# Slot norm statistics moved from GpSimd to VectorE, one token group's norm done earlier, the expert start and a filler moved

## The reference

```python
x = x + _L0_xattn_ref(_layernorm(x, axis=-1), ctx_1024, L0_xattn_Wq, L0_xattn_Wkv, L0_xattn_Wo)
x = x + _L0_ffn_ref(_layernorm(x, axis=-1), L0_ffn_norm_g, ...)
...
def _L0_ffn_ref(x, norm_g, norm_b, slot_g, slot_b, scale, slot_embeds, Wg, bg, Wu, bu, Wd, bd):
    x = _layernorm(x, norm_g, norm_b)
    se = _layernorm(slot_embeds, slot_g, slot_b) * scale
    logits = jnp.einsum('bnd,esd->bnes', x, se)
    dispatch = jax.nn.softmax(logits, axis=1)
    combine = jax.nn.softmax(logits.reshape(x.shape[0], x.shape[1], -1), axis=-1)
    slots = jnp.einsum('bnd,bnes->besd', x, dispatch)
    gate = jax.nn.gelu(jnp.einsum('besd,edf->besf', slots, Wg) + bg[None, :, None, :], approximate=False)
    up = jnp.einsum('besd,edf->besf', slots, Wu) + bu[None, :, None, :]
    eout = jnp.einsum('besf,efo->beso', gate * up, Wd) + bd[None, :, None, :]
    eout = eout.reshape(eout.shape[0], -1, eout.shape[-1])
    return jnp.einsum('bns,bso->bno', combine, eout)
```

## Time and profile before

| | us |
|---|---|
| time, median of 3 runs | 936.28 (935.89 to 938.46) |
| time of the profiled execution | 936.28 |
| its span (first to last instruction) | 934.6 |

### The profile page before, as it was taken

The page is one execution under the profiler, slowest core; times in us unless marked ns, Lnnn a source line. Parts: engine busy times, 40 slices in busy tenths (PEclk is TensorE's granted clock), DMA queues, the critical chain, the costliest instruction groups (busy, mean ns, idle before and its releaser), DMA issues.

```text
span 934.6 us, 16084 instructions
## 1 busy us (share of the span) xinstructions
PE 877.7 (94%) x4768; PEld 675.4 (72%) x4768; DVE 703.1 (75%) x1613; ACT 525.4 (56%) x1008; POOL 584.4 (63%) x575
## 2 busy tenths in 40 slices
PE   7898999999898888999999999999999999998897
PEld 5566666666597856788888888888888676776675
DVE  6997777999645789866666666666668778887866
ACT  3555667544561165666666666666666755446365
POOL 5922444677802245777777777777777778988600
PEclk9999999999999999999999999999999989999998
DMA  7000000322000000200000000000002000000001
GB/s 200 1 2 1 0 2 0 96 68 67 28 2 29 1 9 2 68 26 26 25 25 21 24 25 23 25 25 25 25 21 98 1 1 1 1 1 1 0 13 35
DMA packets 27432, 24.46 MB, mean 26 GB/s; under 512 B 3483, under 2 KB 24179, under 8 KB 27251
## 3 DMA queue, kind: packets, MB, share of 16 engines
q1 hardware_dynamic: 27379, 23.80, 8.6%
HBM read 22.74 MB, written 1.05 MB: 25 GB/s over the span
## 4 chain that ended last, share of the span: by engine, by line
PE 68%; DVE 18%; POOL 6%; ACT 5%; issue 3%; DMA 0%; DVEq 0%; POOLq 0%; ACTq 0%
PE psum L1909 63%; POOL hh L744 3%; DVE arena L1842 2%; ACT hh L876 2%; DVE stats L1369 1%; PE psum L2077 1%; DVE arena L1477 1%; DVE arena L1474 1%; ACT arena L937 1%; PE psum L1970 1%; DVE xn L1388 1%; POOL rstd L655 1%; PE psum L2154 1%; PE psum L1939 1%; DVE arena L1486 1%
## 5 line engine op out<-in xcount | busy, mean ns | idle before, releaser
L1909 PE MATMUL psum<-xw 128*128 128x512 f32 x1248 | 323.0, 394 | 2.6 <-POOL xw L667 1.1
L707 POOL TENSOR_TENSOR hh<-arena,hh 128x512 fp32r<-128x512 f32 x176 | 228.1, 1296 | 81.7 <-ACT hh L876 80.3
L1909 PEld LDWEIGHTS psum<-xw 128*128 128x128 f32 x1248 | 232.2, 188 | 55.1 <-issue 3.8
L1740 DVE TENSOR_TENSOR psum<-psum,arena 128x512 f32<-128x512 f32 x176 | 123.0, 699 | 97.8 <-PE psum L1909 91.5
L1108 ACT ACTIVATE arena<-psum 128x512 f32<-128x512 f32 x176 | 105.4, 599 | 120.3 <-PE psum L1909 120.2
L876 ACT ACTIVATE hh<-arena 128x512 fp32r<-128x512 f32 x228 | 142.3, 625 | 38.5 <-DVE arena L1842 36.1
L1909 PE MATMUL psum<-hh,wdn 128*128 128x512 f32 x528 | 148.3, 389 | 0.2 <-POOL hh L707 0.2
L1745 DVE TENSOR_TENSOR arena<-psum,arena 128x512 f32<-128x512 f32 x176 | 121.7, 691 | 7.6 <-DVE psum L1740 1.7
L1909 PEld LDWEIGHTS psum<-hh,wdn 128*128 128x128 f32 x528 | 98.9, 188 | 21.1 <-POOL hh L707 0.5
L1909 PE MATMUL psum<-arena 128*32 128x128 f32 (+6 forms) x992 | 90.1, 313 | 10.1 <-ACT arena L876 6.8
L876 ACT ACTIVATE arena<-psum 128x512 f32<-128x512 f32 (+6 forms) x85 | 57.4, 687 | 48.6 <-PE psum L1970 18.6
(11 more groups left out here) (296 smaller groups left out, 1494.9 us busy)
## 6 DMA issues: line engine op xcount, KB each, us to landing
egu<-in_w SPq DMA_DIRECT2D x44, 128.0 KB, 2.1
egu<-in_egu SPq DMA_DIRECT2D x16, 256.0 KB, 2.7
edn<-in_w SPq DMA_DIRECT2D x44, 64.0 KB, 1.8
edn<-in_edn SPq DMA_DIRECT2D x16, 128.0 KB, 2.0
arena<-in_w SPq DMA_DIRECT2D x1, 1536.0 KB, 6.5
X<-in_x SPq DMA_DIRECT2D x4, 256.0 KB, 4.2
arena<-in_ctxTd SPq DMA_DIRECT2D x2, 512.0 KB, 5.8
arena<-in_conv SPq DMA_DIRECT2D x1, 768.0 KB, 4.3
```

Of the source, the lines that this page charges most:

```text
L707: pool.tensor_tensor(hh[:, s % 4, 1, :], h1[:, s % 2, :], hh[:, s % 4, 0, :].bitcast(F32), ALU.subtract).then_inc(hh_lo, 1)
L1740: dve.tensor_tensor(bank(2 + k), bank(2 + k), sil[:, k, :], ALU.mult).then_inc(prod_done, 1)
L1909: return pe.matmul(dst, lhsT=lhsT, rhs=rhs, start=start, stop=stop)
```

## The change

- `slot_sums` and its passes leave GpSimd. VectorE makes the slots' statistics at `t == 5` of the attention loop (`slot_stats`: 8 BN_STATS, 8 BN_AGGR, one TENSOR_SCALAR), then `slot_gs`. GpSimd waits for them (`se_var`) and keeps the power, one subtraction and one product.
- Group 3's statistics are made as for other groups, right behind tile 15's residual addition; its power moves to behind step 3 on GpSimd, its application to `q == 6`, its transposes and evacuation to `q == 9`. Group 2's evacuation moves to behind `bexp(0)`.
- `bmax(2)` stands ahead of `brec(0)`.
- At the experts' start VectorE and TensorE wait for all 16 slot evacuations (15 before on VectorE; TensorE's wait stood in `least_T(0)`). ScalarE's first weight copy moves behind the last evacuation, and the Gelu table is no longer loaded ahead of time by a dummy activation.
- `busy(6, 3)` is added at the head of `combine_rows2`.

The first copy and the table load now stand behind the last evacuation. The diff:

```diff
@@ -163,8 +163,8 @@
         ctxTd = carve(B * 2 * C)
         slot_raw = carve(ES // P, D)
         slot_n = carve(ES // P, D)
-        slot_sq = carve(ES // P, D)
-        slot_half = carve(ES // P, D // 2)
+        smv = carve(ES // P, 2)
+        sstats = carve(ES // P, 6)
         srstd = carve(3, ES // P)
         taken[0] = 0
@@ -323,6 +323,7 @@
         ln_xn = sem("ln_xn")
         ln_tp = sem("ln_tp")
         ln_xnT = sem("ln_xnT")
+        se_var = sem("se_var")
         se_n = sem("se_n")
         se_tp = sem("se_tp")
         se_T = sem("se_T")
@@ -798,22 +799,9 @@
                     ln_power(0, 3)
                     for b in range(4, B):
                         keys(b)
-
-                    def slot_sums(rows):
-                        then(pool.tensor_tensor(slot_half, rows[:, :, 0:D // 2], rows[:, :, D // 2:D], ALU.add))
-                        n = D // 4
-                        while n:
-                            then(pool.tensor_tensor(slot_half[:, :, 0:n], slot_half[:, :, 0:n], slot_half[:, :, n:2 * n], ALU.add))
-                            n //= 2
-
-                    pool.wait_ge(w_slots, 16 * N_SLOTS)
-                    slot_sums(slot_raw)
-                    then(pool.tensor_scalar(srstd[:, 2, :], slot_half[:, :, 0], 1.0 / D, None, ALU.mult))
-                    then(pool.tensor_tensor(slot_n, slot_raw, wide(srstd[:, 2, :].unsqueeze(2), ES // P, D), ALU.subtract))
-                    then(pool.tensor_tensor(slot_sq, slot_n, slot_n, ALU.mult))
-                    slot_sums(slot_sq)
-                    then(pool.tensor_scalar(srstd[:, 0, :], slot_half[:, :, 0], 1.0 / D, EPS, ALU.mult, ALU.add))
+                    pool.wait_ge(se_var, 1)
                     then(pool.tensor_tensor(srstd[:, 1, :], srstd[:, 0, :], neghalf[:, 0:ES // P], ALU.pow))
+                    then(pool.tensor_tensor(slot_n, slot_raw, wide(smv[:, :, 0:1], ES // P, D), ALU.subtract))
                     pool.tensor_tensor(slot_n, slot_n, wide(srstd[:, 1, :].unsqueeze(2), ES // P, D), ALU.mult).then_inc(se_n, 1)
                     continue
                 for g in range(NG):
@@ -825,7 +813,7 @@
                         pool.wait_ge(brec_done, k + 1)
                         pool.tensor_tensor(qb[:, k % 4], qb[:, k % 4], wide(recB[:, k % 4].unsqueeze(2), 2, N), ALU.mult)\
                             .then_inc(bnorm_done, 1)
-                        if k == 7:
+                        if k == 3:
                             ln_power(1, NG - 1)
                     experts0_low()
                     pool.wait_ge(xh_lo, E0)
@@ -955,13 +943,6 @@
                                           bias=nmB[:, k % 4, c:c + 1], accum_out=sumB[:, k % 4, c:c + 1])
                 last.then_inc(bexp_done, 1)
-            def gate_up0_high(n, i, k, f):
-
-                act.wait_ge(egu_in[k], i * 16 + 16)
-                if later(n, 2):
-                    act.wait_ge(eu_ready, n - 1)
-                copy(wgu_pair(f, 0), egu_part(k, f)).then_inc(wgu_hi, 1)
-
             def slots_evac(b, hf):
                 act.wait_ge(slots_mm, 2 * b + hf + 1)
                 act.activation(slotsT[:, 8 * hf:8 * hf + 8, b, :], bank(6 + hf).rearrange("p (e s) -> p e s", s=S0), ACT.Identity,
@@ -970,22 +951,26 @@
 
             bexp(0)
+            ln_evac_group(1, 2)
             bexp(1)
             bexp(2)
             for q in range(4 * B + 2):
                 if q + 3 < 4 * B:
                     bexp(q + 3)
-                if q in (4, 14):
-                    ln_evac_group(1, 2 if q == 4 else NG - 1)
-                if q == 4 * B - 4:
-                    gate_up0_high(0, 0, 0, 0)
-                if q == 4 * B - 2:
-                    load_table(ACT.Gelu)
+                if q == 9:
+                    ln_evac_group(1, NG - 1)
                 if q >= 4 and q % 4 == 1:
                     slots_evac(q // 4 - 1, 1)
                 if q % 4 == 3 and q < 4 * B:
                     slots_evac(q // 4, 0)
+
+            def gate_up0_high(n, i, k, f):
+
+                act.wait_ge(egu_in[k], i * 16 + 16)
+                if later(n, 2):
+                    act.wait_ge(eu_ready, n - 1)
+                copy(wgu_pair(f, 0), egu_part(k, f)).then_inc(wgu_hi, 1)
             def gelu(n, e, f):
                 act.wait_ge(eg_ready, n + 1)
@@ -1032,6 +1017,7 @@
                             eo_low(i - 2)
                 row_evac(i)
+            gate_up0_high(0, 0, 0, 0)
             expert_pair(0)
             expert_pair(1)
             with act.Fori(2, E0 // 2 - 1) as i:
@@ -1393,7 +1379,7 @@
                 if L == 7 and t == NT - 1:
                     token_low(0)
-                if t % 4 == 3 and not (L == 1 and t == NT - 1):
+                if t % 4 == 3:
                     if L == 7 and t // 4 == 2:
                         token_integers(0)
                     ln_stats(L, t // 4)
@@ -1448,6 +1434,17 @@
                     .then_inc(xq_lo, 1)
 
+            def slot_stats():
+                dve.wait_ge(w_slots, 16 * N_SLOTS)
+                for t in range(ES // P):
+                    last = dve.bn_stats(sstats[:, t, :], slot_raw[:, t, :])
+                then(last)
+                for t in range(ES // P):
+                    last = dve.bn_aggr(smv[:, t, :], sstats[:, t, :])
+                then(last)
+                dve.tensor_scalar(srstd[:, 0, :], smv[:, :, 1], EPS, None, ALU.add).then_inc(se_var, 1)
+                dve.tensor_scalar(slot_gs[:, :], cols[:, COL["slot_g"]:COL["slot_g"] + 2], scal[:, 0:1], None, ALU.mult).then_inc(se_n, 1)
+
             ln_stats(0, 0)
             ln_apply(0, 0)
             dve.wait_ge(krep_done, 1)
@@ -1478,8 +1475,7 @@
                 if t in (0, 2):
                     ln_stats(0, 2 + t // 2)
                 if t == 5:
-                    dve.wait_ge(w_slots, 16 * N_SLOTS)
-                    dve.tensor_scalar(slot_gs[:, :], cols[:, COL["slot_g"]:COL["slot_g"] + 2], scal[:, 0:1], None, ALU.mult).then_inc(se_n, 1)
+                    slot_stats()
                 if 2 <= t <= NT + 1:
                     u = t - 2
                     dve.wait_ge(av_ready, u + 1)
@@ -1510,17 +1506,15 @@
 
             bmax(1)
+            bmax(2)
             brec(0)
-            bmax(2)
             for q in range(4 * B):
                 if q + 1 < 4 * B:
                     brec(q + 1)
                 qt_evac(q // 4, q % 4)
                 if q + 3 < 4 * B:
                     bmax(q + 3)
-                if q == 4:
-                    ln_stats(1, NG - 1)
-                if q == 10:
+                if q == 6:
                     ln_apply(1, NG - 1)
             def slot_halves(e, k):
@@ -1571,10 +1565,9 @@
                         if f == 0 and k == 0 and later(i, 2):
                             eo_high(i - 2)
-            dve.wait_ge(slots_sb, 2 * B - 1)
+            dve.wait_ge(slots_sb, 2 * B)
             slot_halves(0, 0)
             slot_halves(1, 1)
-            dve.wait_ge(slots_mm, 2 * B)
             least_logits(0)
             expert_pair(0)
             expert_pair(1)
@@ -2100,10 +2093,12 @@
                     dispatch_T(q)
                     if q + 3 < 4 * B:
                         logits_slots(q + 3)
-                if q == 14:
+                if q == 9:
                     ln_transpose(1, NG - 1)
                 if q >= 2:
                     slots_part((q - 2) // 4, (q - 2) % 4 // 2, q % 2)
+
+            pe.wait_ge(slots_sb, 2 * B)
             def gate_up0(n, k, f):
@@ -2127,8 +2122,6 @@
             def least_T(b):
                 pe.wait_ge(least_done, b * 4 + 3)
-                if not later(b, 1):
-                    pe.wait_ge(slots_sb, 2 * B)
                 if later(b, 2):
                     pe.wait_ge(eo_tok[1], b - 1)
                 for a in range(TB):
@@ -2521,6 +2514,7 @@
                 mm(bank(4 + q), w2part(0, c, 1), hh[:, n % 4, 1, :], False, c == NC2 - 1).then_inc(down_done, 1)
             def combine_rows2():
+                busy(6, 3)
                 pe.wait_ge(rw_done, NG + 1)
                 for q in range(2):
                     half = bank(4 + 3 * q).bitcast(BF16)
```

## The result

| | before | changed |
|---|---|---|
| time, median of 5 runs each, us | 936.28 (932.58 to 938.46) | 942.40 (940.88 to 942.61) |
| profiled execution: time, us | 936.28 | 941.85 |
| its span, us | 934.6 | 940.1 |
| mean granted TensorE clock | 0.978 | 0.978 |

The ratio is 1.0065, with a 95% interval from 1.0052 to 1.0079: the changed kernel is slower by 6.1 us, 4.9 to 7.4.

A forecast was written before the change was run, and what follows sets the result against it. VectorE was taken to bound layer 0's attention and the experts' start, TensorE the dispatch loop and layer 5's routing transposes. 1.1 + 0.9 + 2.2 + 0.7 = 4.9 us on 936.28 gave 941.2 us, 8-in-10 range 938.9 to 943.4.

The forecast's parts named there:

- A: Slot statistics on VectorE in layer 0's attention: 1.1 us slower, after the refund from a shorter slot_gs.
- what is added to VectorE here is paid in full: Layer 0's attention: VectorE sets the pace, so its added work costs its full length; GpSimd's work beside it costs nothing.
- the clock rival: TensorE's clock falls in new idles at the dispatch ramp (942.7 us) and experts' start (943.3 us); 22%.
- B: Group 3's norm and bmax order at the dispatch ramp: 1.53 us later, 0.59 refunded, 0.9 us net.
- C: Experts' start: 1.91 us waiting for the 16th evacuation plus 0.3 for copies beside slot halves, 2.2 us; bounds 1.9 and 2.6.
- Table load: Gelu table at the experts' start: its 1.28 us load runs during TensorE's first gate product, cost 0.
- D: Filler busy(6, 3) ahead of layer 5's routing transposes, where TensorE is late: 0.7 us, bounds 0 and 1.3.
- Nothing gives the delay back: Stages between the changed places: no engine waits for something with a fixed time, so the 4.9 us delay stays.
- The overlap at the start: Experts' start: TensorE's 1.13 us idle is slack of the whole stage, so 1.1 us there and 940.1 in all; 14%.
- The clock staying up: Low-clock stretches at 82 to 84 and 778 us vanish: 938.3 us, within 0.3% of before; 12%.

The follow-up runs named there:

- the kernel without C: Changed kernel with VectorE waiting for 15 evacuations again, first weight copy, Gelu table and TensorE's wait at their old places: 939.86 us, ratio 1.0043 to before.
- the kernel without A: Changed kernel with slot statistics back on GpSimd and slot_gs alone on VectorE at t == 5: 939.63 us, ratio 1.0042 to before.

## Why the prediction came out as it did

**Direction, range: right**, and by its mechanism; that the number came so close is partly luck, as the last but one paragraph says. VectorE's added work in layer 0, the shifted ramp and the 16th evacuation are paid one behind the other, and no stage hides one.

**A: mis-sized.** The sum "2.5 + 0.1 - 1.46 = 1.1 us" was right in its own terms (1.18). The step that failed is "what is added to VectorE here is paid in full" taken as all there is to pay. A step of 3.70 us on VectorE is an idle of 2.36 on TensorE, and behind it came half clock in the stage where TensorE has little slack: 1.42 more, and 0.25 at the second stretch. The prediction had the clock rival for the ramp and the experts alone, though the attention loop had the row that showed such a fall.

**B: right**, 1.54 and back 0.6 to 0.67, net 0.87 against 0.9. The clock fall behind the 2.30 us idle is the first rival's; it stands in the changed kernel's profile and that of the kernel without C (0.8 us), and not in three others with the same idle. It was priced at 942.7 - 941.2 = 1.5, twice what it took.

**C: wait right, contention too small.** 1.91 as worked out; 0.3 was taken for the copies beside the slot halves, 0.63 was measured here, with TensorE at half clock, and 1.00 to 1.01 in the four kernels with both copies late and full clock. So the bound of 2.6 for C was too low: at full clock C is 2.9. The clock rival's "at most 0.6" more for a fall at the experts didn't come either: with the fall the stretch was shorter, 5.91 against 6.29. "Between 0 and 0.73 I take 0.3" counted one copy; the pair falls there. The rule of the Trainium skill (SBUF — State Buffer, Who interferes with whom), an exclusive hold by whoever comes first, is nearer: GpSimd's first operation begins at 165.90 and would be done with its 0.73 at 166.63; VectorE's, issued at 166.02, ends at 167.18, 0.55 us behind that. The trace agrees in the order of who waits, and not to the last tenth: a hold to the end would let VectorE's 0.69 us end at 167.32. VectorE pays 0.4 to 0.5 at each collision.

**Table load: right**, no cost. **D:** 0.7 predicted, 0.76 in the row, 0.5 in the difference.

**"Nothing gives the delay back": wrong.** The 7.08 us at `hidden0(0)` are 7.12 at the end of the experts (255.86 against 249.51, and 0.77) and 6.02 at the `up2` products (5.25 + 0.77); with D's 0.50 and 0.26 back behind it they are 6.26 at the end (5.49 + 0.77). In the part where 1.1 came back, both profiles have four stretches' length of half clock, at other places (from 258, 299, 312 and 336 us before; from 263, 317 and, twice as long, 341 in the changed kernel). In the last part the changed kernel has none at 890 us, where the one before has. One stretch cost 0.8 to 1.6 us where it could be read, in the ramp and the attention loop. What the later ones cost was not measured, so that the refund comes from them is likely and not shown; the change edits nothing there but the filler. So the total of 941.2 is near the 942.4 partly by luck: two omissions offset each other, too little in layer 0, at the ramp and at the copies, and nothing given back later.

**The rivals.** The clock fell in the new gaps, the first rival, yet the place where it always fell was the one that rival hadn't named. The overlap at the start falls by the kernel without C. The clock staying up is real in single executions (the kernel without A has no stretch from 19 to 261 us) but did not decide the sign.

## What to carry to other kernels

Work added to the engine that sets the pace is also idle time of TensorE. Add the price of a clock fall to it (here 1.42 us beside 1.18 of work, where TensorE has little slack), and forecast the time with the fall and without it. A tiny operation with a long row that ends with a long one of GpSimd can be a wait; here moving it a few steps took 1.25 of its 1.46 us out of the timeline. Size parts of 1 us by local differences between two timelines; the whole time of a kernel whose unchanged runs differ by 3 us to either side can't tell them.
